# Cross-attention and a block-quantized feed-forward layer on one core: who makes the low halves of twelve hidden rows

## The chip, the cores and the metric

The kernel runs on one core of one Trainium2 chip. The metric is the device time of one execution in microseconds (us), lower is better. The core's engines each run their own instruction list and meet at semaphores: TensorE (PE in the profile; its weight loads are PEld), VectorE (DVE), ScalarE (ACT), GpSimd (POOL) and SyncE (SP), which here issues DMAs. The reader needs no more than that each list is strictly in order: an instruction that waits holds all those behind it on its engine.

## What is computed

Two layers, with residuals, over `x` of 4 x 512 x 512 floats. Cut to what matters here:

```python
x = x + xattn(layernorm(x), ctx, Wq, bq, Wk, bk)          # 4 batches of 512 rows
def mx(t):                                                # along the last dimension, blocks of 32
    scale = max(max|block| / 448, 1e-30)
    return float8_e4m3(t / scale) * scale
def ffn(x2d):                                             # 2048 rows of 512, hidden size 2048
    gate, up = mx(x2d) @ mx(gate_w).T, mx(x2d) @ mx(up_w).T
    h = silu(gate) * up                                   # silu-times-up, 2048 wide
    return mx(h) @ mx(down_w).T
out = x + ffn(layernorm(x))
```

A "row" below is a row tile: 128 of the 2048 rows, one per partition. There are 16 of them, numbered 0 to 15.

## The kernel before

The program has three parts. In the first, up to about 270 us of the profiled execution, the attention of the four batches is worked off together with the quantizing and turning of the weights; its end, which still holds the feed-forward products of rows 0 to 3 of the hidden part, runs to about 304 us. The second part is a loop of "slots", the third a tail for the last four hidden rows.

**A slot.** Slot `r` (r = 4 to 15) makes gate and up of x row `r` and the down product of hidden row `j = r - 4`. TensorE runs 96 matmuls for gate and up (four chunks of 512 hidden columns, 24 matmuls each), then 48 matmuls for the down product of row j. A product of two float32 numbers is made from float16 halves: a value v is split into `hi = float16(v)` and `lo = float16(v - hi)`, and three products hi x hi, hi x lo and lo x hi are summed. So each hidden row needs both halves, and each half has to be transposed before TensorE can take it as weights.

**The path of hidden row j within its slot.** VectorE adds the result of row j - 1 to the residual (`result_of`, L1154), which waits for the down product of row j - 1; then `round_hidden` (L905, L906, L1145, L1146) rounds row j, which lies in the tile W1, 128 x 2048 float32. ScalarE copies it to the high half, float16, in the first half of W2 (`hidden_hi`, L847). VectorE subtracts to make the low half, in the second half of W2 (`hidden_lo`, L1116). SyncE loads the residual and then issues two transposing DMAs, W2 to the tile AT (`turn_hidden`, L356). TensorE waits for both before its down product of row j (L613). The next hidden row is scaled into W1 at the slot's end (`scale_hidden`, L1124 to L1137), and ScalarE makes its absolute values (`hidden_abs`, L839).

**The path of x row r + 1 within slot r.** Statistics on VectorE (L1092, L1095), the inverse deviation on GpSimd (`inverse_std`, L397 to L406), normalizing on ScalarE (`normalize_row`, L826), scaling on VectorE (`scale_row`, L896 to L1103), absolute values on ScalarE (`row_abs`, L831), rounding on VectorE (`round_row`), the high half on ScalarE (`row_hi`, L835), the low half on VectorE (`row_lo`, L1112), and a transposing DMA (L344) to the tile xr.

**The chunks.** For each chunk ScalarE computes silu from the gate (L697) and VectorE multiplies with up (L959, tile h). The order of all these steps on each engine is written out by hand in that engine's `slot` function. The first and the last slot are written apart; in the last, VectorE also works on hidden rows 12 and 13 (`TAIL` is 12). In the tail, TensorE itself transposes rows 12 to 15 and ScalarE splits them (L669).

The order on ScalarE in a slot, which is what the change touches most, reads:

```python
silu_of(4 * r, 0, unscale[:, 0, 0:1])
hidden_hi(j)
silu_of(4 * r + 1, 1, unscale[:, 0, 1:2])
...
silu_of(4 * r + 2, 0, unscale[:, 0, 2:3])
if not last:
    row_abs(r + 1)
    row_hi(r + 1)
silu_of(4 * r + 3, 1, unscale[:, 0, 3:4])
```

Of the kernel before, what the change touches and what calls it, by code (L numbers as in the profile page):

```python
# [30 lines left out]
ALU = mybir.AluOpType  # L31
ACT = mybir.ActivationFunctionType
# [16 lines left out]
ROOM = 64.0  # L49
# [5 lines left out]
def xattn_ffn(nc, x, ctxT, wqT, bq, wkT, bk, gate_w, up_w, down_w, ident, out):  # L55
# [8 lines left out]
    RT = B * LT  # L64
    UNIT = 2048
    GROUPS = UNIT // 512
    RING = LT
# [10 lines left out]
    with ExitStack() as stack:  # L78
        def sb(name, shape, dt):
            return stack.enter_context(nc.sbuf_tensor(name, shape, dt))  # L80
# [4 lines left out]
        def sem(name):  # L85
            return stack.enter_context(nc.semaphore(name))
# [24 lines left out]
        scale = sb("scale", [P, 3, NB], F32)  # L111
        rscale = sb("rscale", [P, NB], F32)
        dscale = sb("dscale", [P, NB], F32)
# [26 lines left out]
        hrpow2 = sb("hrpow2", [P, 1], F32)  # L140
# [74 lines left out]
        habs_ready = sem("habs_ready")  # L215
        hd_ready = sem("hd_ready")
        hhi_ready = sem("hhi_ready")
        hlo_ready = sem("hlo_ready")
        down_ready = sem("down_ready")
        down_taken = sem("down_taken")  # L220
# [40 lines left out]
        TAIL = RT - RING  # L261
# [7 lines left out]
        FIRST, LAST = RING, RT - 1  # L269
# [8 lines left out]
        def hidden_rows(j):  # L278

            return W[(0, 1, 2, 0)[j - TAIL] if isinstance(j, int) and j >= TAIL else 1][:, :]  # L280

        hidden_parts = W[2][:, :].bitcast(F16).rearrange("p (a n) -> p a n", a=2)
# [108 lines left out]
        @block.gpsimd  # L391
        def _(pool):
            own = Steps(pool_step)

            def carry_wait(n):

                nc.gpsimd.tensor_tensor(pool_idle[:, n:n + 1], mhalf[:, 0:1], mhalf[:, 0:1], ALU.mult)  # L397

            def inverse_std(m, n, ready):

                own.done(nc.gpsimd.tensor_scalar(veps[:, 0:n], m[:, :, 1], LN_EPS, 1.0, ALU.add, ALU.mult))
                own.done(nc.gpsimd.tensor_scalar(nmean[:, 0:n], m[:, :, 0], -1.0, 0.0, ALU.mult, ALU.add))
                pool.wait_ge(pool_step, own.value)
                own.done(nc.gpsimd.tensor_tensor(rstd[:, 0:n], veps[:, 0:n], mhalf[:, 0:n], ALU.pow))  # L404
                pool.wait_ge(pool_step, own.value)
                nc.gpsimd.tensor_tensor(nmr[:, 0:n], nmean[:, 0:n], rstd[:, 0:n], ALU.mult).then_inc(ready, 1)  # L406

            def unit_max(b, k):

                pool.wait_ge(smax_ready, 3 * b + (k + 1))  # L410
                carry_wait(1 + k)
                nc.gpsimd.partition_all_reduce(umax[:, k:k + 1], smax[:, k:k + 1], P,
                                               bass.bass_isa.ReduceOp.max).then_inc(umax_ready, 1)

            own.done(nc.gpsimd.memset(mhalf[:, :], -0.5))
            pool.wait_ge(pool_step, own.value)
            unit_max(0, 0)
            pool.wait_ge(stats_ready, 1)
            inverse_std(mv, LT, rstd_ready)
            unit_max(0, 1)  # L420
            pool.wait_ge(stats_ready, 2)
            inverse_std(mv, LT, rstd_ready)
            unit_max(0, 2)
            with pool.Fori(1, B) as b:
                own.enter(b - 1, 3)
                unit_max(b, 0)
                pool.wait_ge(stats_ready, b + 2)
                carry_wait(0)
                inverse_std(mv, LT, rstd_ready)
                unit_max(b, 1)  # L430
                unit_max(b, 2)
                own.leave(B - 1)
            with pool.Fori(0, RT - FIRST) as n:
                own.enter(n, 3)
                pool.wait_ge(xs_ready, n + 1)
                carry_wait(0)
                inverse_std(xmv[:, :].unsqueeze(1), 1, xr_ready)
                own.leave(RT - FIRST)

        @block.tensor  # L440
        def _(pe):
# [223 lines left out]
        def _(act):  # L665
# [163 lines left out]
            def row_abs(r):  # L829
                act.wait_ge(xv_ready, r - (FIRST - 1))  # L830
                nc.scalar.activation(absX, xw, ACT.Abs, scale=MAGIC).then_inc(xabs_ready, 1)  # L831

            def row_hi(r):
                act.wait_ge(xd_ready, r - (FIRST - 1))
                nc.scalar.activation(x_parts[:, 0, :], xw, ACT.Copy).then_inc(xhi_ready, 1)  # L835
# [7 lines left out]
            def hidden_hi(j):  # L843
                act.wait_ge(hd_ready, j + 1)
                if not isinstance(j, int) or j > 0:
                    act.wait_ge(hT_in, 32 * j)
                nc.scalar.activation(hidden_parts[:, 0, :], hidden_rows(j), ACT.Copy).then_inc(hhi_ready, 1)  # L847

            def slot(r, result=True, last=False):
                j = r - RING  # L850
                if result:
                    hidden_abs(j)
# [3 lines that stand above are left out]
                if last:  # L856
                    hidden_abs(TAIL)
                else:
                    normalize_row(r + 1)
                silu_of(4 * r + 2, 0, unscale[:, 0, 2:3])  # L860
                if not last:
                    row_abs(r + 1)
                    row_hi(r + 1)
                silu_of(4 * r + 3, 1, unscale[:, 0, 3:4])

# [10 lines left out]
        def _(dve):  # L876
            own = Steps(dve_step)

            def carry_wait():

                dve.tensor_copy(dve_idle[:, :], bq_sb[:, :])

            def then(instruction):

                own.done(instruction)
                dve.wait_ge(dve_step, own.value)

            def blocks(t):
                return t.rearrange("p (b k) -> p b k", k=BLOCK)

            def each_block(s):
                return s.unsqueeze(2).broadcast_to([P, s.shape[1], BLOCK])
# [218 lines left out]
                dve.wait_ge(xhi_ready, r - (FIRST - 1))  # L1111
                dve.tensor_tensor(x_parts[:, 1, :], xw, x_parts[:, 0, :], ALU.subtract).then_inc(xlo_ready, 1)  # L1112

            def hidden_lo(j):
                dve.wait_ge(hhi_ready, j + 1)
                dve.tensor_tensor(hidden_parts[:, 1, :], hidden_rows(j), hidden_parts[:, 0, :],  # L1116
                                  ALU.subtract).then_inc(hlo_ready, 1)

            def scale_hidden(j):


                rows = h[:, j % RING, :]
                hw = hidden_rows(j)
                then(dve.tensor_reduce(amax[:, :], blocks(rows), AX.X, ALU.max, apply_absolute_value=True))  # L1124
                yield
                then(dve.tensor_scalar(scale[:, 0, :], amax[:, :], 1.0 / FP8_MAX, TINY, ALU.mult, ALU.max))
                then(dve.tensor_reduce(smax[:, 0:1], scale[:, 0, :], AX.X, ALU.max))
                power_of_two(hpow2[:, :], hrpow2[:, :], smax[:, 0:1])
                dve.tensor_scalar(dscale[:, :], scale[:, 0, :], hrpow2[:, 0:1], -ROOM, ALU.mult, ALU.mult)
                then(dve.reciprocal(rscale[:, :], scale[:, 0, :]))  # L1130
                if isinstance(j, int) and j == TAIL + 2:
                    dve.wait_ge(hT_in, 32 * TAIL)
                elif isinstance(j, int) and j == TAIL + 3:
                    dve.wait_ge(turned, group(tail_unit(TAIL), 4)[1])
                elif not isinstance(j, int):
                    dve.wait_ge(hlo_ready, j)
                dve.tensor_tensor(blocks(hw), blocks(rows), each_block(rscale[:, :]), ALU.mult).then_inc(hv_ready, 1)  # L1137
                yield

# [20 lines left out]
            def slot(r, result=True, last=False):  # L1160
                def chunk(c):
                    hidden_of(4 * r + c, c % 2, h[:, r % RING, c * 512:(c + 1) * 512], unscale[:, 1, c:c + 1])

                if result:
                    result_of(r - (RING + 1))
                    dve.wait_ge(down_taken, r - RING)
                    round_hidden(r - RING)
                if not last:
                    stats_of_row(r + 1)
                chunk(0)  # L1170
                hidden_lo(r - RING)
                chunk(1)
                if last:
                    all_of(scale_hidden(TAIL))
                    round_hidden(TAIL)
                    chunk(2)
                    all_of(scale_hidden(TAIL + 1))
                    chunk(3)
                else:
                    scale_row(r + 1)  # L1180
                    chunk(2)
                    round_row(r + 1)
                    row_lo(r + 1)
                    chunk(3)
                    all_of(scale_hidden(r - (RING - 1)))
# [50 lines left out]
```

## Time and profile before

| | |
|---|---|
| time, median of 2 runs | 741.31 us (740.08 and 742.54) |
| span of the profiled execution, first to last instruction | 738.1 us, 3.2 us under that median |
| PE busy | 671.8 us, 91% of the span |
| DVE busy | 572.5 us, 78% |
| ACT busy | 275.5 us, 37% |
| POOL busy | 64.7 us, 9% |
| mean granted TensorE clock | 0.956 |

The page does not give the profiled execution's time apart from its span. Times in the sections below are microseconds from the start of the span. The slots run from 303.8 us to 675.2 us; the tail takes the rest.

### The profile page before, as it was taken

Reading aid. Unit: us, or ns where it says so; the run is one execution under the profiler, and the core shown is the slowest. Engines: PE = TensorE matmul, PEld = TensorE weight load, DVE = VectorE, ACT = ScalarE, POOL = GpSimd, SP = SyncE. Lnnn points to the kernel's source line nnn. Section 1 sums busy time; section 2 is a strip of 40 time slices with the busy share of each in tenths; the row PEclk is TensorE's granted clock in tenths of the full one; section 3 lists DMA queues with packets and bytes.
Section 4 is the critical chain, followed back from the end, with each engine's and each line's share of the span. In section 5 each row is a group of like instructions: output and inputs, shape, how many; then the busy total and the mean of one; then the engine's idle time right before and its main releaser. Section 6 shows DMA issues by size and latency. Waiting matters only on the chain.

```text
span 738.1 us, 8721 instructions
## 1 busy us (share of the span) xinstructions
PE 671.8 (91%) x2964; PEld 316.9 (43%) x2964; DVE 572.5 (78%) x735; ACT 275.5 (37%) x380; POOL 64.7 (9%) x112
## 2 busy tenths in 40 slices
PE   4394788998997999999999999999999999997997
PEld 1152334544543544444444444444444444443453
DVE  4847789798878877768787697877868787689981
ACT  2354546645744845313132222322223123213342
POOL 0401001002002000101011010100101011000000
PEclk9696599998999999999999999999999999999899
DMA  7023101151131211323140422404133140330111
GB/s 274 0 58 143 57 1 57 58 199 57 57 136 63 71 40 47 51 51 85 43 99 14 99 68 60 99 15 99 48 79 72 42 99 19 81 86 1 44 42 43
DMA packets 80033, 50.88 MB, mean 69 GB/s; under 512 B 64016, under 2 KB 64656, under 8 KB 79504
## 3 DMA queue, kind: packets, MB, share of 16 engines
q1 hardware_dynamic: 80016, 50.67, 25.3%
q8 instruction: 9, 0.15, 0.1%
q14 instruction: 8, 0.07, 0.0%
HBM read 26.54 MB, written 8.39 MB: 47 GB/s over the span
## 4 chain that ended last, share of the span: by engine, by line
PE 47%; issue 24%; DVE 15%; ACT 4%; DMA 4%; POOL 3%; SPq 3%; POOLq 0%; DVEq 0%; ACTq 0%
PE AB L613 21%; PE G L468 19%; DVE W L906 3%; DVE W L905 3%; DMA AT<-W 3%; PE AB L537 2%; SPq L356 2%; DVE W L1146 2%; PE TB L444 2%; DVE W L1116 2%; ACT W L847 2%; PE AB L444 1%; POOL rstd L404 1%; DVE X L1154 1%; DVE W L1137 1%
## 5 line engine op out<-in xcount | busy, mean ns | idle before, releaser
L468 PE MATMUL G<-gu_hi,xr 128*128 128x512 f16 x768 | 231.8, 379 | 1.3 <-DVE h L959 1.3
L613 PE MATMUL AB<-dn_hi,AT 128*128 128x512 f16 x512 | 158.8, 383 | 4.0 <-ACT AT L669 3.2
L468 PE MATMUL G<-gu_lo,xr 128*128 128x512 f16 x384 | 145.5, 379 | 0.0
L468 PEld LDWEIGHTS G<-gu_hi,xr 128*128 128x128 f16 x768 | 75.2, 98 | 95.5 <-DVE h L959 6.2
L613 PE MATMUL AB<-dn_lo,AT 128*128 128x512 f16 x256 | 98.0, 383 | 0.0
L468 PE MATMUL G<-gu_hi,xT 128*128 (+1 forms) x256 | 86.2, 404 | 10.5 <-DVE h L959 9.6
L613 PEld LDWEIGHTS AB<-dn_hi,AT 128*128 128x128 f16 x512 | 50.4, 99 | 64.2 <-DMA AT<-W 5.8
L905 DVE SCALAR_TENSOR_TENSOR W<-absW,W 128x2048 f32<-128x2048 bf16 x28 | 64.1, 2289 | 8.1 <-ACT absW L839 4.7
L839 ACT ACTIVATE absW<-W 128x2048 bf16<-128x2048 f32 x16 | 30.6, 1910 | 103.9 <-DVE W L1137 103.9
L906 DVE SCALAR_TENSOR_TENSOR W<-absW,W 128x2048 f32<-128x2048 bf16 x28 | 64.2, 2292 | 1.0
L537 PE MATMUL AB<-AT,R 128*128 128x512 f32 x128 | 58.3, 596 | 2.2 <-ACT AT L669 2.2
L1154 DVE SCALAR_TENSOR_TENSOR X<-AB,odown,X 128x128 f32<-128x128 f32 x64 | 18.0, 344 | 53.4 <-PE AB L613 53.3
L468 PEld LDWEIGHTS G<-gu_lo,xr 128*128 128x128 f16 x384 | 37.6, 98 | 44.0
L697 ACT ACTIVATE silu<-G,unscale 128x512 f32<-128x512 f32 x48 | 32.3, 675 | 53.3 <-PE G L468 53.3
L468 PE MATMUL G<-gu_lo,xT 128*128 (+1 forms) x128 | 51.6, 403 | 0.0
L959 DVE SCALAR_TENSOR_TENSOR h<-G,unscale,silu 128x512 f32 (+1 forms) x48 | 36.0, 749 | 17.7 <-PE G L468 15.3
L468 PEld LDWEIGHTS G<-gu_hi,xT 128*128 128x128 f16 x256 | 26.3, 103 | 46.4 <-DVE h L959 12.1
L847 ACT ACTIVATE W<-W 128x2048 f16<-128x2048 f32 x12 | 22.9, 1910 | 60.7 <-DVE W L1146 60.7
L397 POOL TENSOR_TENSOR pool_idle<-mhalf 128x1 f32<-128x1 f32 x27 | 5.2, 194 | 452.9 <-DVE xmv L1095 318.9
L444 PE MATMUL TB<-idf,W 128*128 128x128 f32 x256 | 36.7, 284 | 6.9 <-DVE W L947 6.7
L444 PEld LDWEIGHTS TB<-idf,W 128*128 128x128 f32 x256 | 32.2, 148 | 17.3 <-DVE W L947 7.2
L613 PEld LDWEIGHTS AB<-dn_lo,AT 128*128 128x128 f16 x256 | 25.3, 99 | 29.5 <-issue 1.1
(106 smaller groups left out, 825.6 us busy)
## 6 DMA issues: line engine op xcount, KB each, us to landing
W<-in_gate_w SPq DMA_DIRECT2D x4, 1024.0 KB, 5.5
X<-in_x SPq DMA_DIRECT2D x4, 1024.0 KB, 5.3
W<-in_up_w SPq DMA_DIRECT2D x4, 1024.0 KB, 7.9
W<-in_down_w SPq DMA_DIRECT2D x4, 1024.0 KB, 4.8
x_dram<-X SPq DMA_DIRECT2D x4, 1024.0 KB, 4.4
X<-x_dram SPq DMA_DIRECT2D x16, 256.0 KB, 2.8
out_y<-X SPq DMA_DIRECT2D x16, 256.0 KB, 2.0
W<-x_dram SPq DMA_DIRECT2D x12, 256.0 KB, 2.8
```

Of the source, the lines that this page charges most:

```text
L356: sp.dma_start_transpose(hT[:, part, :, :], hidden_parts[:, part, :]).then_inc(hT_in, 16)
L444: last = pe.matmul(dst[:, j * P:(j + 1) * P], t, idf[:, :], is_transpose=True, start=(j == 0), stop=(j == 3))
L468: last = pe.matmul(dst[:, :], a[:, j * P:(j + 1) * P], w[:, j, g, chunk, :], start=(m == 0), stop=(m == 3 * HT - 1))
L537: last = pe.matmul(AB[lt % 2][:, :], XT[:, lt % 2, j * P:(j + 1) * P], AT[:, j, :], start=(j == 0), stop=(j == HT - 1))
L613: last = pe.matmul(down_bank(j)[:, :], hT[:, a, k, :], (dn_hi, dn_lo)[w][:, k, :], start=(k == 0 and a == 0 and w == 0), stop=(k == IT - 1 ...
L697: nc.scalar.activation(silu[:, pair, :], G[2 * pair][:, :], ACT.Silu, scale=factor).then_inc(silu_ready, 1)
L839: nc.scalar.activation(absW[:, :], hidden_rows(j), ACT.Abs, scale=MAGIC).then_inc(habs_ready, 1)
L847: nc.scalar.activation(hidden_parts[:, 0, :], hidden_rows(j), ACT.Copy).then_inc(hhi_ready, 1)
L905: then(dve.scalar_tensor_tensor(v, av, MAGIC_FLOOR, v, ALU.max, ALU.add))
L906: last = dve.scalar_tensor_tensor(v, av, MAGIC_FLOOR, v, ALU.max, ALU.subtract)
L959: dve.scalar_tensor_tensor(dst, G[2 * pair + 1][:, :], factor, silu[:, pair, :], ALU.mult, ALU.mult).then_inc(h_ready, 1)
L1154: last = dve.scalar_tensor_tensor(row_out[:, cols], down_bank(j)[:, cols], odown_of(j)[:, n:n + 1], row_out[:, cols], ALU.mult, ALU.add)
```

## The change

The low half of hidden rows 0 to 11, the twelve of the slots, is made in another way. ScalarE writes the high half with its sign turned (`scale=-1.0`), GpSimd issues a DMA that adds this half to the row in W1 (float16 source, 128 x 2048, added onto float32 in SBUF), which leaves the remainder v - hi in W1, and ScalarE copies the remainder, its sign turned again, into the low half. `dscale` has its sign turned for these rows, so that both halves end with the signs of before. VectorE's subtraction is gone. On GpSimd the DMA of hidden row j is issued between the `inverse_std` of x row j + 4 and that of x row j + 5. VectorE waits for the low half of row j before it overwrites W1, as before, and now at the end of slot 4 and in slot 15 as well.

```diff
-            with pool.Fori(0, RT - FIRST) as n:
-                own.enter(n, 3)
+
+            def row_std(n):
                 pool.wait_ge(xs_ready, n + 1)
                 carry_wait(0)
                 inverse_std(xmv[:, :].unsqueeze(1), 1, xr_ready)
-                own.leave(RT - FIRST)
+
+            def hidden_rest(j):
+
+                pool.wait_ge(hhi_ready, j + 1)
+                if not isinstance(j, int):
+                    carry_wait(1)
+                nc.gpsimd.dma_start(hidden_rows(j), hidden_parts[:, 0, :],
+                                    accum_op=ALU.add).then_inc(hrest_in, 16)
+
+            row_std(0)
+            with pool.Fori(1, RT - FIRST) as n:
+                own.enter(n - 1, 3)
+                hidden_rest(n - 1)
+                row_std(n)
+                own.leave(RT - FIRST - 1)
+            hidden_rest(TAIL - 1)
...
-                nc.scalar.activation(hidden_parts[:, 0, :], hidden_rows(j), ACT.Copy).then_inc(hhi_ready, 1)
+                nc.scalar.activation(hidden_parts[:, 0, :], hidden_rows(j), ACT.Copy, scale=-1.0).then_inc(hhi_ready, 1)
+
+            def hidden_lo(j):
+                act.wait_ge(hrest_in, 16 * j + 16)
+                nc.scalar.activation(hidden_parts[:, 1, :], hidden_rows(j), ACT.Copy, scale=-1.0).then_inc(hlo_ready, 1)
...
                 if not last:
                     row_abs(r + 1)
+                hidden_lo(j)
+                if not last:
                     row_hi(r + 1)
                 silu_of(4 * r + 3, 1, unscale[:, 0, 3:4])
...
-            def hidden_lo(j):
-                dve.wait_ge(hhi_ready, j + 1)
-                dve.tensor_tensor(hidden_parts[:, 1, :], hidden_rows(j), hidden_parts[:, 0, :],
-                                  ALU.subtract).then_inc(hlo_ready, 1)
-
...
-                dve.tensor_scalar(dscale[:, :], scale[:, 0, :], hrpow2[:, 0:1], -ROOM, ALU.mult, ALU.mult)
+                dve.tensor_scalar(dscale[:, :], scale[:, 0, :], hrpow2[:, 0:1],
+                                  -ROOM if isinstance(j, int) and j >= TAIL else ROOM, ALU.mult, ALU.mult)
...
-                elif not isinstance(j, int):
+                elif not isinstance(j, int) or j == 1:
                     dve.wait_ge(hlo_ready, j)
+                elif j == TAIL + 1:
+                    dve.wait_ge(hlo_ready, TAIL)
...
                 chunk(0)
-                hidden_lo(r - RING)
                 chunk(1)
```

On ScalarE, in the loop over the slots, the rows from the normalizing of x row r + 1 to the last silu of the slot were these (G0 and G2 hold gates, R2 the x row, R1 its absolute values, W0 its halves):

```order
L826 ACTIVATE R2<-W0,nmr,rstd 128x512
L696 REGISTER_ALU
L697 ACTIVATE silu<-G0,unscale 128x512
L831 ACTIVATE R1<-R2 128x512
L835 ACTIVATE W0<-R2 128x512
L696 REGISTER_ALU
L697 ACTIVATE silu<-G2,unscale 128x512
```

and are now these, with line numbers of the changed file (+16):

```order
L842 ACTIVATE R2<-W0,nmr,rstd 128x512
L712 REGISTER_ALU
L713 ACTIVATE silu<-G0,unscale 128x512
L847 ACTIVATE R1<-R2 128x512
L866 ISA
L867 ACTIVATE W2<-W1 128x2048
L851 ACTIVATE W0<-R2 128x512
L712 REGISTER_ALU
L713 ACTIVATE silu<-G2,unscale 128x512
```

The low half of the hidden row (L867, behind a wait, L866) stands behind the absolute values of x row r + 1 and ahead of that row's high half and the slot's last silu.

On GpSimd, in the loop over the slots, one turn was this:

```order
L397 ISA
L397 TENSOR_TENSOR pool_idle<-mhalf 128x1
L401 TENSOR_SCALAR veps<-xmv 128x1
L402 TENSOR_SCALAR nmean<-xmv 128x1
L403 ISA
L404 TENSOR_TENSOR rstd<-veps,mhalf 128x1
L405 REGISTER_ALU
L406 TENSOR_TENSOR nmr<-nmean,rstd 128x1
```

and is now this:

```order
L398 TENSOR_TENSOR pool_idle<-mhalf 128x1
L445 DMA W1<-W2 128x2048
L436 REGISTER_ALU
L398 TENSOR_TENSOR pool_idle<-mhalf 128x1
L402 TENSOR_SCALAR veps<-xmv 128x1
L403 TENSOR_SCALAR nmean<-xmv 128x1
L404 ISA
L405 TENSOR_TENSOR rstd<-veps,mhalf 128x1
L406 REGISTER_ALU
L407 TENSOR_TENSOR nmr<-nmean,rstd 128x1
```

The DMA and the wait for the high half of hidden row j come ahead of the statistics of x row j + 5, so these can no longer start before that high half is made.

## Rows read from the trace of the kernel before

**Rows 1.** The page, part 1: busy time, share of the span, instructions of TensorE.

```profile
PE 671.8 (91%) x2964; PEld 316.9 (43%) x2964; DVE 572.5 (78%) x735; ACT 275.5 (37%) x380; POOL 64.7 (9%) x112
```

**Rows 2.** Stretches from one down product to the next: busy times, clock, DMA.

```profile
476.42:507.81 31.39, 31.34 (x145) 13.87 (x145) 24.78 (x33) 8.31 (x9) 3.13 (x5) 1.00 0.30 67
```

**Rows 3.** The chain that ended last, one slot: start, us, what.

```profile
486.96 1.14 DVE X L1154 x4
...
488.21 2.30 DVE W L905
...
490.54 2.30 DVE W L906
...
493.13 2.30 DVE W L1146
...
495.54 1.92 ACT W L847
...
497.48 2.30 DVE W L1116
...
500.43 2.92 SPq L356
...
503.40 4.37 DMA AT<-W
```

**Rows 4.** Waits from 350 to 634 us: who, for whom, total us, times, longest.

```profile
PEld AB L613 <- DMA AT<-W: 5.5, 10, 0.8
```

**Rows 5.** Timeline of the same slot, ScalarE, GpSimd and VectorE: the x row.

```profile
499.86 0.81 ACT L826 ACTIVATE R<-W,nmr,rstd 128x512 f32<-128x512 f32 x1 [1.83 <-POOL nmr L406]
...
502.72 0.63 ACT L831 ACTIVATE R<-R 128x512 bf16<-128x512 f32 x1 [1.48 <-DVE R L1103]
...
496.38 0.19 POOL L397 TENSOR_TENSOR pool_idle<-mhalf 128x1 f32<-128x1 f32 x1 [27.91 <-DVE xmv L1095]
...
497.82 2.00 POOL L406 TENSOR_TENSOR nmr<-nmean,rstd 128x1 f32<-128x1 f32 x1
...
500.70 0.69 DVE L896 TENSOR_REDUCE xamax<-R 128x16 f32<-128x512 f32 x1 [0.27 <-ACT R L826]
```

**Rows 6.** DMA issues: queue, count, KB each, median us from issue to landing.

```profile
W<-in_up_w SPq DMA_DIRECT2D x4, 1024.0 KB, 7.9
...
W<-in_down_w SPq DMA_DIRECT2D x4, 1024.0 KB, 4.8
x_dram<-X SPq DMA_DIRECT2D x4, 1024.0 KB, 4.4
X<-x_dram SPq DMA_DIRECT2D x16, 256.0 KB, 2.8
```

**Rows 7.** Timelines and chain of the first slot, ScalarE, SyncE and TensorE.

```profile
303.12 1.91 ACT L847 ACTIVATE W<-W 128x2048 f16<-128x2048 f32 x1 [2.49 <-DVE W L1146]
...
307.83 6.42 SPq L356 DMA_TRANSPOSE AT<-W  x2
...
319.51 10.38 PE AB L613 x48
```

**Rows 8.** The chain in the last slot and the first of the tail.

```profile
661.51 2.30 DVE W L1137
663.83 1.92 ACT absW L839
...
679.82 1.91 ACT absW L839
```

**Rows 9.** Stretches around two gaps of TensorE; the third last number is the clock.

```profile
231.08:234.48 3.40, 0.00 (x1) 0.01 (x1) 3.07 (x3) 0.00 (x0) 0.00 (x0) 0.93 0.00 0
234.48:237.22 2.74, 2.74 (x7) 1.03 (x8) 2.74 (x3) 1.45 (x4) 2.07 (x3) 0.50 0.00 0
679.05:682.27 3.22, 0.01 (x2) 0.01 (x1) 3.22 (x3) 2.45 (x3) 0.00 (x0) 0.83 0.00 0
682.27:688.00 5.73, 5.73 (x14) 2.24 (x15) 5.59 (x5) 1.03 (x2) 0.00 (x0) 0.50 0.00 0
```

More of the change, by code:

```diff
@@ L217, in xattn_ffn @@
         hhi_ready = sem("hhi_ready")
+        hrest_in = sem("hrest_in")
         hlo_ready = sem("hlo_ready")
```

## Prediction

> **What bounds the kernel now.** I read the page first: TensorE is busy for 91% of the span [rows 1], so in general only what TensorE waits for counts. Then the windows from one down product to the next: a slot takes 31.4 us, TensorE is busy in 31.34 of them at full clock, VectorE in 24.78, ScalarE in only 8.31 and GpSimd in 3.13 [rows 2]. That looks like a loop bound by TensorE with a helper at 79% that could be relieved by one at 26%. But busy shares do not say how much room the hidden row has, so the third view is the chain of waits [rows 3]. In about half of the slots it runs not through TensorE's 96 products but through the hidden row: the result of row j - 1 at 486.96 us, three long VectorE passes of 2.30, ScalarE's high half (1.92, to 497.46), VectorE's low half (2.30, to 499.78), SyncE's issue of the transposes (from 500.43) and their landing at 503.40 + 4.37 = 507.77. The down product before ended at 486.93 and the next starts at 507.81: 20.9 us. TensorE's 96 products between them take 31.4 - 10.5 = 20.9 us too. The two paths are equal to a few tenths, and the waits say the same: before each of ten down products TensorE's weight load waited 0.5 us on average for the transposes [rows 4]. So the hidden row has **no slack in the middle slots**: whatever is added between the high half and the transposes is added to the slot. The path starts anew at the end of each down product, so nothing can be caught up by working ahead.
>
> **Part 1: VectorE's subtraction goes.** It frees 12 x 2.29 = 27.5 us of VectorE and takes 2.32 us (2.30 and a gap of 0.02) from the hidden path of each slot [rows 3]. On VectorE the room itself is worth nothing in the middle slots: what follows there is the multiplication of chunk 1 and then the x row, which is not late. It matters in the last slot (part 5).
>
> **Part 2: a DMA from GpSimd takes its place on the hidden path.** It starts when ScalarE's high half is done (497.46), behind a wait and an idle operation of 0.19 us [rows 5], 0.25 with the gaps. The trace has no accumulating DMA and none from GpSimd, so its time L from there to landing needs bounds. The nearest rows are plain DMAs from SyncE: 256 KB in 2.8 us; 1024 KB, the size that is written here, in 4.4 to 7.9 [rows 6]. This DMA reads 512 KB of float16 and 1024 KB of the old row, adds with a conversion, and writes 1024 KB. Lower bound: a plain 1024 KB store, 4.4. Upper bound: the two reads and the write in turn at 4.4 each, 13. The straight line through 256 KB at 2.8 and 1024 KB at 4.6 gives some 2.2 + 2.3 per MB, which for the 1.5 MB read is 5.7, with nothing for the adding, the conversion and descriptors made in software. I take **L = 8.0**, the slowest plain row of this size (7.9), and keep 4.4 and 13 for the range.
>
> The Trainium skill ("DMA: Bandwidth & Descriptors", section "Anatomy of one DMA — SWDGE (gpsimd) path") fits such DMAs by 2.0 us plus bytes over 436 GB/s. By it L would be, as an estimate, 4.4 us for the 1 MB written and 5.6 for the 1.5 MB read, and the sum would be that of rival 1; no row here shows a DMA of this kind.
>
> **Part 3: ScalarE's low half follows.** 128 x 2048 from float32 to float16 is what its high half does in 1.92 us, so I take 1.92 and a gap of 0.04 [rows 3]. The middle slot becomes longer by 0.25 + 8.0 + 1.96 - 2.32 = **7.9 us**. The transposes behind it keep their 8.0 us from the low half's end to landing. Queued behind the waiting ScalarE instruction are the x row's high half and the slot's last silu, and behind these VectorE's `row_lo`, chunk 3 and the scaling of the next hidden row (some 6.5 us). They end near 516 us here and are needed by TensorE or by the next slot's rounding no earlier than 515.7 + 10.5 = 526, so that wait is covered. SyncE's transposes of the x row also move behind the hidden ones by 8 us, and are needed at 526 too.
>
> **Part 4: the order on GpSimd and ScalarE sets a floor.** The low half stands behind `row_abs(r + 1)` on ScalarE, and that row's inverse deviation now stands behind the DMA on GpSimd. Before, GpSimd started it at 496.38 [rows 5]. Now it starts after the high half and the issue, at 497.7 + q. No row gives q, the time for which an issue holds GpSimd; I take 1 us and keep 0 and 2. The four small operations then take 1.65: the last of them, 2.00 us long, ran beside VectorE's subtraction [rows 5], which is gone, and I give it the 0.19 of its like. Then come normalizing 0.81, scaling 2.0 (from 500.70 to the end of the multiplication at 502.69), absolute values 0.63, gaps 0.15: together 5.25. ScalarE cannot begin the low half before 497.7 + 1 + 5.25 = 504.0. With L = 8 the DMA lands at 505.7 and decides; with any L under 6.3 the order decides, and the slot grows by 504.0 + 1.96 - 499.78 = 6.2 us (5.2 to 7.2 with q). So a quick DMA does not make the change cheap.
>
> **The clock.** TensorE now stands still for some 7.9 us ahead of each down product. The trace shows what follows shorter gaps: after 3.40 us without a matmul (231.08 to 234.48) the granted clock was at 0.50, the 1.2 GHz level, for the next 2.74 us, and after 3.22 us (679.05 to 682.27) for the next 5.73, and then full again [rows 9]. At half clock dense matmuls lose half of the stretch: 1.4 to 2.9 us a gap. The down product lies on the path, so each middle slot pays this; I take 2.2. A middle slot thus grows by 7.9 + 2.2 = **10.1 us**.
>
> **Part 5: the sum.** Rows 1 to 10 of the hidden rows sit in middle slots: 10 x 10.1 = 101 us. *Row 0* has slack. Its high half ended at 305.0, its transposes were issued at 307.83, with their queue entry 1.5 us longer than in the middle slots (6.42 against 4.97), so they landed at 315.2 to 316.6, while TensorE came to the down product at 319.51 [rows 7]: of 7.9 some 3.6 is covered, 4.3 left, and 2.0 for the clock, 6.3 us. *Row 11*, in the last slot: VectorE goes on to chunk 1 some 1.6 us earlier; ScalarE's order is then the absolute values of row 12, which ended at 663.83 + 1.92 [rows 8] and now end at 664.1, a silu (0.65), the low half from 664.8 to 666.7. It was 657.0 before, so the down product of row 11 is 9.4 us later (0.3 is slack), and 2.2 longer for the clock. Against that, TensorE waited in the tail until 682.27 for VectorE's scaling of row 13 and its absolute values (1.91 from 679.82) [rows 8], then at half clock for 5.73 us. VectorE is early now, so that wait shrinks by 3.3 and the 2.9 of the clock go: 9.4 + 2.2 - 3.3 - 2.9 = 5.4 us. Sum 101 + 6.3 + 5.4 = 113 us, span 738.1 + 113 = 851. The profiled span lies 3.2 us under the median, so I say **854 us**.
>
> **Rivals.** *1. The DMA is quick and the order decides.* L of 4.4 to 6.3: 10 x (6.2 + 1.4 to 2.2) + row 0 with 2.6 + 1.7 + row 11 with 5.4 gives 86 to 94 us, 827 to 835. For it: the 4.4 us rows. Against: none of them adds or converts. *2. The DMA is slow.* L = 13: 10 x (12.9 + 2.5) + 9.3 + 2.3 + 8.5, the last since the low half then starts 3 us later in the last slot too: 174 us, 915. For it: two reads and an addition. *3. The clock holds.* Without the 2.2 us per gap 854 becomes 829. Against it stand both gaps of rows 9. *4. Not slower.* The mechanism would be slack in the transposes: if their 7.4 us from issue to landing were mostly a wait for TensorE to read AT, and not their own time, a later low half would shorten them. It needs 7.9 us of such slack to come out level, and would then give 741, or 739 with the last slot's earlier VectorE. In row 0's slot they had nothing to wait for and their queue entry was longer, not shorter [rows 7], so I hold it near impossible. That the change does not do what it says is excluded by the order of instructions.
>
> A rule that speaks of a further cost: in the trace a GpSimd operation of one element took 2.00 us while VectorE subtracted two SBUF tiles [rows 5], against 0.19 for its like. The Trainium skill ("SBUF — State Buffer", section "Who interferes with whom") says that a VectorE instruction with two SBUF inputs contends with GpSimd's reads, and that VectorE's 2-port modes stop its descriptor writing. By the rule the DMA's issue would be held up to 2.3 us (a pass of that size) where such an instruction runs beside it; from 497.7 us VectorE has only chunk 1, with an input in PSUM, so I add nothing.
>
> **Chances and range.** The forecast, a DMA that lands 6.3 to 10 us after its start with the clock falling, 838 to 878 us: 0.42. Rival 1: 0.25. Rival 2 and all above 10 us: 0.20, of which 0.08 above 905. Rival 3: 0.10, down to 815 where the order decides too. Rival 4: 0.01; something else 0.02. The range that leaves out less than 0.2 is **815 to 905**. About 2% is what a measurement can tell here, and even the cheapest case is 10% slower: slower 0.98, same 0.01, faster 0.01.
>
> **What the profile after would show.** Busy VectorE down by 27.5 us, ScalarE up by 23; slots of 41.5 us in place of 31.4; in each a gap of about 8 us ahead of L613, released by the transposes, and after it matmuls at clock 0.50 for 3 to 6 us; in the chain of waits a DMA onto W of 8 us, then ScalarE's copy, in every middle slot and TensorE's products in none. If the low half follows `row_abs` at once, rival 1 holds; if it waits for the DMA, L can be read from it. What would make me wrong is L above all: each microsecond is worth ten or eleven. A long q would do the same through the floor.

## The result, and the profile after

The changed kernel takes 832.13 us (median of 2 runs, 831.59 and 832.68) against 741.31: a ratio of 1.1235, 95% interval 1.1172 to 1.1299, so slower by 91 us. The profiled execution took 831.59 us with a span of 829.8.

The page, part 1 (to compare with [rows 1]), and the DMA that is new in part 6 (DMA issues: count, KB each, median us from issue to landing):

```profile
PE 693.5 (84%) x2964; PEld 321.8 (39%) x2964; DVE 546.1 (66%) x723; ACT 296.7 (36%) x392; POOL 57.9 (7%) x135
...
W<-W POOLq DMA_DIRECT2D x12, 1024.0 KB, 5.8
```

VectorE is busy for 26.4 us less, ScalarE for 21.2 more: that part of the change did what it says. TensorE has the same 2964 matmuls and yet is busy for 21.7 us *longer*, a first sign that they ran slower. The profile page's chain of waits is of little use here: it enters GpSimd's list and puts 73% of the span down to "issue". So the reading goes by the waits and the timeline. Who waited, from 350 to 730 us, the lines that answer to [rows 4]:

```profile
PEld AB L629 <- DMA AT<-W: 63.4, 10, 6.8
PE AB L629 <- DMA AT<-W: 58.5, 10, 6.3
```

TensorE stood still for 5.9 us on average before each of ten down products; before the change its weight loads had waited for 0.5 us there. The last slot, outside this window, has the longest wait, 9.3 us; row 0's was 3.1. One middle slot on ScalarE, GpSimd and SyncE (answers to [rows 3, 5]):

```profile
541.38 1.91 ACT L863 ACTIVATE W<-W 128x2048 f16<-128x2048 f32 x1 [5.30 <-DVE W L1166]
...
546.10 0.81 ACT L842 ACTIVATE R<-W,nmr,rstd 128x512 f32<-128x512 f32 x1 [2.24 <-POOL nmr L407]
...
548.97 0.63 ACT L847 ACTIVATE R<-R 128x512 bf16<-128x512 f32 x1 [1.48 <-DVE R L1125]
549.51 1.89 ACT L867 ACTIVATE W<-W 128x2048 f16<-128x2048 f32 x1
...
543.37 0.19 POOL L398 TENSOR_TENSOR pool_idle<-mhalf 128x1 f32<-128x1 f32 x1 [36.10 <-ACT W L863]
543.50 0.90 POOL L445 DMA_DIRECT2D W<-W  x1
...
545.88 0.19 POOL L407 TENSOR_TENSOR nmr<-nmean,rstd 128x1 f32<-128x1 f32 x1
...
552.06 4.82 SPq L357 DMA_TRANSPOSE AT<-W  x2
```

The high half starts at 541.38 and the low half at 549.51, 8.13 us later. The low half has no bracket: ScalarE did not sit idle before it but came straight from the absolute values of the x row (L847). Yet the DMA, sent at 543.50, lands after 5.8 us, at 549.3. The absolute values and the DMA end within about 0.2 us of each other. The 8.13 us are the measure for the experiments: call it **d**, from the start of the high half to the start of the low half. The low half is complete 1.9 us after d; before the change VectorE had it complete at 4.24 (from 495.54 to 499.78 [rows 3]), so it is 5.8 us late, which is TensorE's wait.

Windows of the same slot, of its gap, and of the two parts of the down product behind the gap (as [rows 2, 9]; the third last number is the clock); the last row is the down product of hidden row 0:

```profile
532.80:572.66 39.86, 34.16 (x145) 14.63 (x144) 22.57 (x32) 10.10 (x10) 2.39 (x7) 0.91 0.34 79
553.60:559.31 5.71, 0.01 (x2) 0.01 (x1) 5.27 (x9) 0.00 (x0) 0.00 (x0) 0.90 1.07 216
559.31:565.12 5.81, 5.81 (x14) 2.08 (x15) 1.41 (x1) 1.91 (x1) 0.00 (x0) 0.51 0.28 73
565.12:572.60 7.48, 7.48 (x36) 3.43 (x35) 0.00 (x0) 0.00 (x0) 0.00 (x0) 1.00 0.00 0
324.48:335.00 10.52, 10.52 (x49) 4.79 (x50) 3.74 (x7) 1.91 (x1) 0.00 (x0) 1.00 0.16 41
```

After a gap of 5.7 us the first 5.8 us of the down product ran at 0.51, the 1.2 GHz level, and did the work of some 2.9. This is one of the longer stretches: in the slot whose down product starts at 401.54, behind a gap of 5.85 us, the clock was at 0.50 for the first 3.0 us and at 1.00 for the next 3.0. The middle slots differ by this, 38.5 to 40.2 us from one down product's start to the next. Behind row 0's gap, 3.06 us long, the clock stayed at 1.00.

The sum over the program, by the start of VectorE's result (L1154, now L1174) as a mark: row 0's result 335.05 against 329.91, later by 5.1, of which the part ahead of the slots already had 1.9 (scatter: in the traces of the experiments that keep this DMA its first issue lies between 305.4 and 308.8 us, 307.1 in this one); from there to the result of row 10, 394.8 against 314.5, 80.4 in ten slots, **8.0 each**; from there to the end 99.9 against 93.7, 6.2. Together 91.7.

### The profile page after: what moved, and what is told of

It is laid out like the page before. It is cut to its first block, busy times and chain, and to the rows that moved or that the text cites. A ratio compares the mean times of both kernels' runs of the same rounds, so it can differ in the third digit from the quotient of the medians.

```text
span 829.8 us, 8740 instructions
## 1 busy us (share of the span) xinstructions
PE 693.5 (84%) x2964; PEld 321.8 (39%) x2964; DVE 546.1 (66%) x723; ACT 296.7 (36%) x392; POOL 57.9 (7%) x135
## 4 chain that ended last, share of the span: by engine, by line
issue 73%; PE 7%; DVE 7%; POOL 6%; ACT 3%; DMA 2%; SPq 1%; POOLq 0%; DVEq 0%
PE AB L629 5%; POOL rstd L405 2%; DVE W L928 1%; DVE W L927 1%; POOL pool_idle L398 1%; POOL nmean L403 1%; DMA AT<-W 1%; POOL veps L402 1%; PE AB L553 1%; SPq L357 1%; ACT absW L855 1%; DMA idf<-in_ident 1%; PE AB L460 1%; DVE W L1166 1%; DVE W L1157 1%
## 5 line engine op out<-in xcount | busy, mean ns | idle before, releaser
L629 PE MATMUL AB<-dn_hi,AT 128*128 128x512 f16 x512 | 174.8, 417 | 71.7 <-DMA AT<-W 70.9
L629 PEld LDWEIGHTS AB<-dn_hi,AT 128*128 128x128 f16 x512 | 54.1, 106 | 144.3 <-DMA AT<-W 76.8
L1174 DVE SCALAR_TENSOR_TENSOR X<-AB,odown,X 128x128 f32<-128x128 f32 x64 | 18.0, 344 | 137.0 <-PE AB L629 136.9
L629 PE MATMUL AB<-dn_lo,AT 128*128 128x512 f16 x256 | 106.6, 416 | 0.0
L398 POOL TENSOR_TENSOR pool_idle<-mhalf 128x1 f32<-128x1 f32 x38 | 10.3, 270 | 536.2 <-ACT W L863 391.5
L629 PEld LDWEIGHTS AB<-dn_lo,AT 128*128 128x128 f16 x256 | 27.1, 106 | 34.1 <-issue 9.4
```

The lines of the kernel that those rows point to most:

```text
L629: last = pe.matmul(down_bank(j)[:, :], hT[:, a, k, :], (dn_hi, dn_lo)[w][:, k, :], start=(k == 0 and a == 0 and w == 0), stop=(k == IT - 1 ...
L1174: last = dve.scalar_tensor_tensor(row_out[:, cols], down_bank(j)[:, cols], odown_of(j)[:, n:n + 1], row_out[:, cols], ALU.mult, ALU.add)
```

## Experiments

All times are medians against the kernel before on the same chip (741.3 in the first two sets, 741.0 in the third); d is read from one middle slot of each trace, and "waits" is TensorE's total wait for the transposes in all twelve slots unless another number of slots is given; it was 70.9 us in the changed kernel.

### 1. Is the low clock a cost of its own?

The gap ahead of each down product is filled with 24 matmuls that nobody needs.

```diff
+                if not result:
+                    pe.wait_ge(lo_ready, group(UNITS - 1, 3)[1] + 1)
+                for _ in range(24):
+                    pe.matmul(TB[0][:, :], dn_hi[:, 0, 0:P], gu_hi[:, 0, 0, 0, :], start=True, stop=True)
                 pe.wait_ge(hT_in, 32 * j + 32)
```

> The changed kernel, with 24 matmuls of 128x512 whose results nobody reads, issued by TensorE between its products and its wait for the transposed halves, in each of the 12 slots. They fill 24 x 0.215 = 5.2 us of a gap that is now 5.7 to 6.3 us long. Theory (the stall costs twice: its own length, and the low clock behind it): the granted clock stays at 1.00 in the down products, which take 10.5 us again in place of 13.1 or so; 2.2 us a slot less, 12 slots: 806 us. Rival (the clock is no cost of its own, the path through the halves sets the time whatever TensorE's speed is): 832 us or, if the fill delays the down product, more.

Measured 811.12 us, 21.0 less than the changed kernel. The filling did not delay the down products, which still waited 0.7 us each for the transposes (7.1 us in ten slots), and the clock holds:

```profile
345.00:700.00 355.00, 347.87 (x1599) 154.72 (x1598) 216.39 (x309) 98.43 (x99) 23.86 (x70) 1.00 0.37 87
```

The mean of a down product's matmul on the high half is 383 ns again, as before the change; it was 417. So the clock is a cost of its own, 21 us in the ten middle slots. The expected 26 us counted rows 0 and 11 in full. Row 0 had none, and row 11's was not removed: 24 matmuls fill 5.2 of its 9.3 us, a gap of 4.37 us was left, and the first 5.98 us behind it ran at 0.60 on average. What is left of the cost, 70 us over the kernel before, is as large as the changed kernel's waits (70.9).

### 2. The DMA's landing or the order on ScalarE?

Three kernels: the low half ahead of the absolute values; the DMA over half of the columns; both. The two with half of the DMA leave out the remainder of the other 1024 columns, so their results are wrong there; they serve to read times only.

```diff
-                if not last:
-                    row_abs(r + 1)
                 hidden_lo(j)
                 if not last:
+                    row_abs(r + 1)
                     row_hi(r + 1)
```

```diff
-                nc.gpsimd.dma_start(hidden_rows(j), hidden_parts[:, 0, :],
+                nc.gpsimd.dma_start(hidden_rows(j)[:, 0:UNIT // 2], hidden_parts[:, 0, 0:UNIT // 2],
```

> The changed kernel, with ScalarE's low half placed ahead of the absolute values of the next x row, in place of behind them. In the trace the DMA lands 5.8 us after its start, at 549.3, and the absolute values end at 549.5, so two conditions tie. Theory A (both decide, each 0.2 us from the other): nothing gained, 829 to 832 us. Theory B (the order alone decides, as the prediction's first rival had it, and the halves could start when silu ends at 547.5): 2.0 us a slot, 808 us.

> The changed kernel, but the accumulating DMA covers only the first 1024 of the 2048 columns, so that the remainder is not made for the others; the order on all engines as changed. The DMA should land 1.5 to 2 us sooner. Theory A (tie) and theory B (order): the absolute values of the x row still end at 549.5, so nothing is gained: 828 to 832 us. Theory C (the DMA's landing alone decides): 1.7 us a slot, 812 us.

> Both edits: the DMA covers only the first 1024 columns, and the low half stands ahead of the absolute values. Theory A (a tie of landing and order): only with both removed does the slot shorten, by 1.5 to 2 us: 808 to 814 us. If the time stays at 830, the DMA's time is not in its bytes, or something else holds the low half.

Measured 831.08, 830.56 and 806.75 us. Neither edit alone gains more than 1.6 us; both together gain 25.4, a little more than the 18 to 24 expected. The low half's rows in the three traces:

```profile
548.18 1.91 ACT L867 ACTIVATE W<-W 128x2048 f16<-128x2048 f32 x1 [1.75 <-DMA W<-W]
```

```profile
547.67 1.89 ACT L867 ACTIVATE W<-W 128x2048 f16<-128x2048 f32 x1
```

```profile
572.24 1.91 ACT L867 ACTIVATE W<-W 128x2048 f16<-128x2048 f32 x1
```

Their high halves started at 540.32, 539.54 and 566.13, so d is 7.86, 8.13 and 6.11. In the first ScalarE sat idle for 1.75 us until the DMA landed; in the second it came straight from the absolute values, although the DMA landed after 3.9 us in place of 5.8; in the third it came straight from the silu ahead of it, which ended at 572.24, and the DMA (issued at 568.24, 3.9 us) had landed at 572.1. So these 6.11 us are again two conditions within 0.1 us of each other, and taking away more of either alone would gain nothing. TensorE's waits were 68.9, 71.3 and 50.5 us, against 70.9. A tie is shown: two conditions, 0.2 us apart, and each edit removed one. The last slot is not in this: there the low half waits behind the absolute values of hidden row 12 in all three kernels, and TensorE's wait of 9.2 to 9.5 us did not move. The DMA took 1.9 us less for half of the bytes; the straight line through the two sizes leaves 2.0 us that do not depend on them.

The Trainium skill ("DMA: Bandwidth & Descriptors", section "Anatomy of one DMA — SWDGE (gpsimd) path") fits such a DMA by 2.0 us plus bytes over 436 GB/s. With the 1.5 MB that it reads as the bytes, that is an estimate of 5.6 us for the whole and 3.8 for the half; measured were 5.8 and 3.9. With the 1 MB that it writes the estimate would be 4.4, which the trace does not bear out.

### 3. The same path with no DMA in it

VectorE makes the remainder in place, and ScalarE the low half, first with the order as changed, then with the order freed.

```diff
-                nc.gpsimd.dma_start(hidden_rows(j), hidden_parts[:, 0, :],
-                                    accum_op=ALU.add).then_inc(hrest_in, 16)
...
                 chunk(0)
+                dve.wait_ge(hhi_ready, r - RING + 1)
+                dve.tensor_tensor(hidden_rows(r - RING), hidden_rows(r - RING), hidden_parts[:, 0, :],
+                                  ALU.add).then_inc(hrest_in, 1)
                 chunk(1)
```

and in the second kernel also

```diff
-                hidden_rest(n - 1)
                 row_std(n)
+                hidden_rest(n - 1)
...
+                hidden_lo(j)
                 silu_of(4 * r + 2, 0, unscale[:, 0, 2:3])
```

> The changed kernel without the DMA: VectorE adds the negated high half onto the row in place (float32, between chunk 0 and chunk 1, where its subtraction stood), and ScalarE makes the low half at its changed place. GpSimd keeps its wait for the high half ahead of the x row's inverse deviation. So the remainder is there 2.3 us after the high half in place of 6.0. Theory (the order holds the low half as much as the DMA does): the low half still follows the absolute values, which come sooner only by the time of the DMA's issue, 0.7 to 0.9 us: 8 to 12 us less, 820 to 824 us. Rival (the DMA's 5.8 us are the cost): 3.7 us a slot, 788 us.

> As the run without the DMA, and with the order freed: GpSimd makes the x row's inverse deviation without waiting for the high half, and ScalarE makes the low half ahead of the slot's third silu. What is left of the change on the hidden row's path is ScalarE's pass of 1.96 us. Theory: TensorE waits some 2 to 2.5 us a slot, at full clock or nearly (no gap of this length in the trace lowered it): 741 + 12 x 2.0 = 765 us, 760 to 775. Rival (without the DMA the path has room for ScalarE's pass): 741 us.

Measured **849.38 us**, and 778.52; both expectations were missed. In the first, a remainder that is there 3.7 us *sooner* made the kernel 17 us slower, where 8 to 12 us less were expected from the missing issue of the DMA. The trace shows what the expectation left out, GpSimd in that slot and VectorE beside it:

```profile
551.42 2.44 POOL L398 TENSOR_TENSOR pool_idle<-mhalf 128x1 f32<-128x1 f32 x2 [37.02 <-ACT W L862]
...
555.10 0.19 POOL L407 TENSOR_TENSOR nmr<-nmean,rstd 128x1 f32<-128x1 f32 x1
...
551.38 2.29 DVE L1191 TENSOR_TENSOR W<-W 128x2048 f32<-128x2048 f32 x1 [0.31 <-ACT W L862]
```

Two idle operations of 0.19 us took 2.44 together, as long as VectorE's pass beside them. The x row's inverse deviation is 1.2 us later than with the DMA, and by the order on ScalarE so is the low half: d = 558.73 - 549.44 = 9.29. The order decides even with the remainder long there. TensorE's waits were 84.6 us, 13.7 more than in the changed kernel, which is the larger part of the 17.

In the freed kernel:

```profile
550.43 2.00 POOL L407 TENSOR_TENSOR nmr<-nmean,rstd 128x1 f32<-128x1 f32 x1
...
552.47 0.81 ACT L841 ACTIVATE R<-W,nmr,rstd 128x512 f32<-128x512 f32 x1 [1.83 <-POOL nmr L407]
553.18 1.89 ACT L866 ACTIVATE W<-W 128x2048 f16<-128x2048 f32 x1
```

d is 553.18 - 548.15 = 5.03, the low half's end is 2.7 us later than before the change, and TensorE waited 27.9 us in ten slots, 2.8 each. This is ScalarE's pass (1.96) and 0.8 more: GpSimd's last operation again took 2.0 us beside VectorE's pass, and held ScalarE's normalizing ahead of the low half. That is 8 us of the 13.5 over the expected 765. The other part is the last slot, where 2.0 us had been counted and TensorE waited 10.4: the low half came behind the absolute values of hidden row 12 (it started at 697.43, 12.9 us after its high half), though the remainder was there at 688.8. So the order that was freed in eleven slots was not freed in the twelfth.

### 4. Does a VectorE pass hold GpSimd's operations, and the DMA too?

```diff
                 chunk(0)
+                dve.wait_ge(hhi_ready, r - RING + 1)
+                dve.tensor_tensor(absW[:, :], spare(0), spare(1), ALU.add)
                 chunk(1)
```

`spare` is a float32 view of a part of the tile of gate and up weights; the DMA and everything else stay as changed.

> The changed kernel, with one more pass on VectorE in each slot, which nobody needs: an addition of two float32 tiles in SBUF, 128 x 2048, 2.3 us, between chunk 0 and chunk 1, started by the high half as the DMA is. Its result goes to the tile of absolute values, which is free then. Theory (a VectorE pass with two SBUF inputs holds GpSimd's operations that read SBUF, as the 2.00 us operation of the trace of before and the 2.4 us of the run without the DMA suggest): the idle operation ahead of the DMA's issue ends some 2.1 us later, so does the DMA, and each slot: 12 x 2.1 = 25 us more, 857 us. Rival (those operations were long for another reason, or the DMA is sent before the pass begins): 832 us.

Measured 851.03 us, 19 more than the changed kernel. GpSimd and VectorE in one slot:

```profile
552.30 2.30 POOL L398 TENSOR_TENSOR pool_idle<-mhalf 128x1 f32<-128x1 f32 x1 [36.08 <-ACT W L863]
554.54 0.90 POOL L445 DMA_DIRECT2D W<-W  x1
...
552.25 2.29 DVE L1195 TENSOR_TENSOR absW<-gu_hi 128x2048 bf16<-128x2048 f32 x1 [0.31 <-ACT W L863]
```

The idle operation took 2.30 us in place of 0.19, the DMA was sent 2.1 us later, and d is 560.55 - 550.31 = 10.24, 2.1 more. TensorE's waits grew by 23.3 us (94.2 against 70.9); its down matmuls were busy 4.9 us less, so these gaps of some 8 us cost no more clock than those of 5.9. The two make 18.4 of the 19 us. The DMA's own time, 5.8 us, did not change; here it was sent as the pass ended, so this says nothing of a DMA issued during one. That part was not tried.

The Trainium skill ("SBUF — State Buffer", section "Who interferes with whom") says that a VectorE instruction with two SBUF inputs contends with a GpSimd instruction that reads SBUF. This trace agrees: 2.30 us beside such a pass, 0.19 without.

### 5. Taking the transposed halves one by one

TensorE needs the low half only for the last of the three products. The high half's transpose is issued when that half is made, and the down product begins with its 32 matmuls (6.9 us). TensorE's part of the edit is shown; SyncE's loop over the slots is written out as well, in both kernels.

```diff
-                pe.wait_ge(hT_in, 32 * j + 32)
+                pe.wait_ge(hT_hi, 16 * j + 16)
...
                 for g in range(GROUPS):
-                    down_pass(j, g, ((0, 0), (0, 1), (1, 0)))
+                    down_pass(j, g, ((0, 0), (0, 1)))
+                pe.wait_ge(hT_in, 16 * j + 16)
+                for g in range(GROUPS):
+                    down_pass(j, g, ((1, 0),))
```

> The changed kernel, DMA and order as they are, but TensorE takes the transposed halves one by one: the high half's transpose is issued as soon as that half is made, and the down product runs its 32 matmuls on it (6.9 us) before it waits for the low half; then the 16 on the low half. SyncE's slots are written out one after the other. TensorE's wait for the low half was 5.7 to 6.3 us, which the 6.9 us cover: the slots are bound by TensorE again, 31.4 us each. The last slot is 1 us late, and the tail gains 2 to 4 us since VectorE is early: 736 to 744 us. Rival (the two transposes get in each other's way or in the way of the accumulating DMA, or the hidden path is longer by the new order): above 760 us.

> The kernel before, with the same taking of the halves one by one. TensorE waited 0.5 us in the middle slots for the transposes at most, nearly all beside its own work, so there is little to win in the slots: 738 to 742 us, the same within the measurement. It is the control for the run before: the difference between the two is what the change costs or brings once its latency is covered; I expect the change at 0 to 3 us under this one, by VectorE's earlier start in the last slot.

Measured 737.43 us for the changed kernel so edited (ratio to before 0.9944, 0.9927 to 0.9961) and 739.57 for the kernel before with the same edit (0.9975, 0.9960 to 0.9990). The 91 us are gone. Both kernels lie within the 2% under which two times count as the same here. One slot of the first, and its wait for the DMA, from 350 to 730 us:

```profile
614.32:645.70 31.38, 31.38 (x146) 14.07 (x145) 22.64 (x33) 10.11 (x10) 2.39 (x7) 1.00 0.41 92
```

```profile
ACT W L872 <- DMA W<-W: 23.8, 10, 2.5
...
PEld AB L630 <- DMA AT<-W: 0.2, 1, 0.2
```

TensorE is busy through the slot at full clock. The hidden path did not get shorter, it got longer: the DMA now takes 8.4 us to land, beside the high half's transpose, ScalarE waits for it, and d is 571.16 - 560.58 = 10.58. All of it lies beside TensorE's work. The low half is now complete 8.2 us later than before the change, which is more than the 6.9 us of the 32 matmuls. What stands behind it has become shorter: one transposing DMA on SyncE's queue (2.99 us) in place of two (4.97), and that leaves some 6.2 us to cover, an estimate.

### 6. The stall in the tail, and the pair once more

In the tail ScalarE makes the absolute values of hidden row 13 between the high and the low half of the first group of row 12's blocks, and TensorE waits for the low one. The edit moves them behind both halves, in the kernels of experiment 5.

```diff
-                    if step == (0, 0, 1, -1)[j - TAIL]:
+                    if step == (1, 0, 1, -1)[j - TAIL]:
```

> The changed kernel with the halves taken one by one, and one step of the tail's order on ScalarE moved: the absolute values of hidden row 13 come behind both halves of row 12's first group, in place of between them. In the run without this step TensorE stood still for 3.2 us for that pass and then ran at the low clock for 5.7 us. Theory (the pass in between is the cause): the wait goes, and with it the low clock, 3.2 + 2.9 us, less about 1 us since row 13's rounding starts 0.6 us later and is wanted about when it ends: 732 us, 730 to 735. Rival (the wait only moves to row 13's first transpose): 736 to 738 us.

> The kernel before with the same two edits, the control for the run before. By the pair of runs without the tail's step (737.4 and 739.6 us) the change is worth 0 to 2 us once its latency is covered. Theory (VectorE's earlier start in the last slot counts only where TensorE waits for it): 732 to 736 us, the same as its partner within a few tenths of a per cent.

Measured 736.90 us (0.9948, 0.9927 to 0.9969) and 740.21 (0.9979, 0.9966 to 0.9992). The theory of some 5 us fell: neither differs from its version without the step by more than the scatter. It rested on a misreading. The stall of 3.2 us with the low clock behind it is that of the kernel before [rows 9]; in the trace of the changed kernel of experiment 5 the stall at that place was 1.64 us, with the clock at 1.00 on both sides. With the step, TensorE:

```profile
679.47 0.39 PE L476 MATMUL TB<-AT,neg_id 128*128 128x512 f16 x1 [0.77 <-ACT AT L689]
...
694.42 1.04 PE L630 MATMUL AB<-dn_hi,AT 128*128 128x512 f16 x4 [2.67 <-ACT AT L689]
```

The second of these waits was 1.80 us without the step. So 1.64 and 1.80 became 0.77 and 2.67, the same 3.44 us: the wait only moved, as the rival said, and the larger part of it to row 14's absolute values, which stand between the halves of row 13's first group.

The pair tells more: in the two comparisons the change is 2.1 and 3.3 us better than its control. The intervals of the two ratios just overlap in either pair (by 0.0001 and 0.0003), so this is small and likely, not certain. The traces show a place for a part of it. TensorE waits longer in the controls for the absolute values of row 13, 3.26 in place of 1.64 us and 2.40 in place of 0.77, so 1.6 us in either pair. That this comes from VectorE's pass, which the controls still have in the last slot, is likely and was not tried by itself. The second control also ran at 0.56 for the 2.8 us behind its stall of 2.67, which its partner did not.

## Why the prediction came out as it did

The direction, the place and the kind of cost were right, and the time (854 forecast, 832 measured) lies in the range of 815 to 905, though under the 838 to 878 that the forecast itself was given. Of the 22 us between, most are one term, the DMA's time. By its steps:

- **No slack on the hidden row's path.** Right, and what the forecast hung on. TensorE's wait of 5.85 us a slot is the 5.8 us by which the low half is late; with the slack made by experiment 5 the whole cost was gone.
- **Part 2, the DMA's time L.** This term was mis-sized: 8.0 taken, 5.8 measured. The straight line through the two plain DMAs with the read bytes, 5.7, was the better estimate; the prediction took the slowest plain row of this size in its place, with the adding and the conversion in mind. The measured time leaves next to nothing for these two, though no run takes them away by themselves.
- **Part 4, the floor by the order.** It became the rule, as rival 1 said: by the traces of experiment 2 it ties with the DMA. Predicted start of the low half 504.0 in the coordinates of the slot of before; measured 495.54 + 8.13 = 503.7. The floor's price was 6.2 us a slot; measured 5.85. q, put at 1, is 0.6 to 0.7 (the DMA's issue begins at 543.50, GpSimd's next operation at 544.16), and that idle operation took 0.46 in place of 0.19.
- **Part 3, ScalarE's pass.** Right: 1.89 to 1.91 us.
- **The clock.** 2.2 us a middle slot taken; 8.0 less the wait of 5.85 is 2.2, a mean of slots with some 3 and slots with up to 6 us at the low clock. Experiment 1 got back 21 us in these ten slots. For row 0 it was wrong: after a gap of 3.06 us the clock held, where 2.0 had been charged. The length of a gap does not settle this. Besides the two gaps in [rows 9], 3.2 and 3.4 us, with 0.50 behind them, row 0's gap of 3.22 us in experiment 4 had 0.55 behind it for 3.0 us, and of the ten gaps of 2.6 to 3.1 us in the freed kernel of experiment 3 one, of 2.80 us, had 0.55 for 3.0 us and nine had 1.00. The control of experiment 5 kept 1.00 behind a gap of 3.26.
- **The sum.** Ten middle slots 80.4 (101 forecast; at rival 1's sizes 84), row 0 3.2 (6.3), last slot and tail 6.2 (5.4), and 1.9 of scatter ahead of the slots. In the last slot the low half was forecast 12.0 us after the start of its high half and came after 11.8 (750.09 - 738.26). The sum of rival 3 is 1 us off: 854 less 22, 2.0 and 2.2 is 828. Rival 1's time, 827 to 835, is the measured one; it was given 0.25 and deserved more, since the bounds of L reached to both sides of its threshold, 6.3, and the one estimate worked out from rows lay under it.
- **The rule on VectorE and GpSimd.** Nothing was added, rightly for this kernel: VectorE was idle from 543.0 to 544.0, then had chunk 1, and the idle operation ahead of the issue took 0.19. Experiment 4 shows what a pass in the freed place costs by way of GpSimd: 2.1 us a slot.
- **What the profile would show.** Slots of 39.5 on average, not 41.5; gaps of 5.9 us, not 8, and behind them the low clock for 3 to 6 us as listed; VectorE down by 26.4 (27.5 forecast) and ScalarE up by 21.2 (23). The chain of waits did not show the DMA, and its 5.8 us are read from the list of issues. The low half followed `row_abs` at once, the sign that was named for rival 1.

## What to carry to other kernels

Before work is moved to an idle engine, ask whether the path through it has slack at the consumer, not whether the source engine is busy: here TensorE waited for the length of the hidden row's path and not for room on VectorE, and 26 us of relief cost 91. The same latency was free once the consumer took its operands in the order in which they come: 32 of the 48 matmuls needed only the high half. And where a new wait seems to decide, look for the condition that ends just beside it; an edit that removes one of two tied conditions gains nothing and can look like proof that it did not matter; only the edit that removes both shows what they hold.

## What was not expected of the hardware

- An accumulating DMA within SBUF, float16 onto float32 128 x 2048, took 5.8 us from issue to landing, and 3.9 for half of the columns: by the line through the two, 2.0 us and 3.8 for the full size. GpSimd's next operation began 0.66 us after the issue. Beside a transposing DMA of 512 KB it took 8.4 us.
- One-element operations on GpSimd took 2.0 to 2.3 us in place of 0.19 beside a VectorE pass of 2.29 us with two SBUF inputs (2.44 for two of them), and the DMA issued behind them was late by that, 2.1 us, with its own 5.8 us unchanged.
- Granted clock behind gaps on TensorE: behind the ten gaps of 5.6 to 6.3 us of the changed kernel it was at 0.50 for some 3 to 6 us, and behind those of some 8 us no longer than that. Behind gaps of 2.6 to 3.3 us it was at 1.00 in most cases (3.06, 3.26) and at 0.50 to 0.55 in some (2.80, 3.22). Matmuls that nobody needs, put in the gap, kept it at 1.00 and gave back 21 us.
